# The prologue of an attention stage: another order of the first batch's work, of the stores and of the hand-over of PSUM banks

## The reference, cut to what matters

```python
x = x + attention(layernorm(x), w_in, offsets, amplitudes, sharpness)
x = x + ffn(layernorm(x), ...)
x = x + mamba(layernorm(x), ...)
x = x + ffn(layernorm(x), ...)

def attention(x, w_in, offsets, amplitudes, sharpness):   # x: 2 x 1024 x 128, 16 heads of 8
    proj = einsum('bld,ed->ble', x, w_in)
    k, v, q = heads(proj[..., :d]), heads(proj[..., d:2*d]), heads(proj[..., 2*d:])
    diff = offsets[:, :, None] - rel          # rel = -(L-1) .. L-1
    scores = sum(amplitudes * exp(-abs(sharpness) * diff * diff), axis=1)
    bias = scores[:, i - j + L - 1]
    attn = softmax(q @ k.T / sqrt(8) + bias)
    return attn @ v
```

## Time and profile before

| | us |
|---|---|
| median of 3 runs (lowest, highest) | 1184.79 (1184.17, 1186.43) |
| the profiled execution | 1184.06 |
| its span, first to last instruction | 1182.1 |
| PE busy in the span | 1020.0 |
| DVE busy | 983.5 |
| ACT busy | 719.0 |
| POOL busy | 447.7 |

### The profile page before, as it was taken

How to read it: one execution, slowest core, us unless ns; L and a number is a source line. 1 busy time by engine, 2 the same in 40 slices (tenths; PEclk the granted TensorE clock), 3 DMA queues, 4 the chain that set the end, 5 groups by cost and what they waited for, 6 DMA issues and landing times. The chain is left out here.

```text
span 1182.1 us, 19693 instructions
## 1 busy us (share of the span) xinstructions
PE 1020.0 (86%) x5756; PEld 540.9 (46%) x5756; DVE 983.5 (83%) x2432; ACT 719.0 (61%) x1175; POOL 447.7 (38%) x404
## 2 busy tenths in 40 slices
PE   3559999999999999785999999782877769999998
PEld 1212222222222222264766676541656537666775
DVE  6589999889999986168999999787876689999997
ACT  5116665666666656564777777586333537777775
POOL 4600000000000000013777778515663127777776
PEclk9659999999999999967999999986889879999999
DMA  3740122032012200000000000000000000000001
GB/s 100 255 95 8 61 76 49 16 106 66 15 55 75 57 1 2 1 21 12 20 21 18 22 18 23 3 19 0 1 0 0 21 9 21 22 18 21 19 23 38
DMA packets 56704, 41.66 MB, mean 35 GB/s; under 512 B 23334, under 2 KB 51004, under 8 KB 56636
## 3 DMA queue, kind: packets, MB, share of 16 engines
q1 hardware_dynamic: 54268, 38.18, 12.0%
q10 hardware_dynamic: 2368, 2.63, 0.8%
HBM read 33.12 MB, written 7.47 MB: 34 GB/s over the span
## 5 line engine op out<-in xcount | busy, mean ns | idle before, releaser
L514 POOL TENSOR_TENSOR f_act_low<-f_act,f_act_high 128x512 fp32r<-128x512 f32 x256 | 331.2, 1294 | 151.3 <-ACT f_act_high L471 146.3
L1203 ACT ACTIVATE at_prob<-at_cols 128x1024 f32<-128x1024 f32 x256 | 248.1, 1021 | 198.4 <-PE at_cols L1092 198.4
L1255 DVE CUSTOM_DVE_ANT_0 at_rows<-at_rows,at_table_max 128x512 f32<-128x512 f32 x512 | 340.3, 719 | 33.5 <-PE at_rows L1057 32.3
L471 ACT CAST f_act_high<-f_act 128x512 fp32r<-128x512 f32 x256 | 159.1, 621 | 68.1 <-DVE f_act L591 65.7
L585 DVE TENSOR_TENSOR f_gated<-f_relu,f_work 128x512 f32<-128x512 f32 x256 | 174.3, 681 | 21.3 <-PE f_work L417 15.1
L591 DVE TENSOR_TENSOR f_act<-f_gated,f_work 128x512 f32<-128x512 f32 x256 | 175.8, 687 | 10.2
L478 ACT ACTIVATE f_relu<-f_work 128x512 f32<-128x512 f32 x256 | 152.9, 597 | 32.1 <-PE f_work L362 30.7
L360 PE MATMUL f_work<-f_x_high,f_wu_high 128*128 128x512 f32 x256 | 148.4, 580 | 2.7 <-DVE f_wu_low L573 2.1
L1057 PE MATMUL at_rows<-at_k_stack,at_q_stack 48*128 48x512 bf16 x512 | 104.7, 405 | 39.9 <-DVE at_maxima L1255 38.4
L1104 PE MATMUL at_pv<-at_prob,at_v_stack 128*32 128x512 f32 x1024 | 136.4, 605 | 0.6 <-ACT at_prob L1203 0.6
L1092 PE MATMUL at_cols<-at_table_cols,flip_sum 128*64 128x512 f16 x1024 | 136.4, 387 | 0.0
(11 more groups left out here) (274 smaller groups left out, 1393.8 us busy)
## 6 DMA issues: line engine op xcount, KB each, us to landing
at_table_cols<-bias_rows SPq DMA_DIRECT2D x32, 248.0 KB, 5.1
at_table_max<-bias_rows SPq DMA_DIRECT2D x12, 480.0 KB, 4.3
f_wu<-in_L_ffn_up_w_dram SPq DMA_DIRECT2D x64, 64.0 KB, 2.0
f_wd<-in_L_ffn_down_w_dram SPq DMA_DIRECT2D x64, 64.0 KB, 1.8
at_q_stack<-q_parts SPq DMA_DIRECT2D x28, 96.0 KB, 2.4
at_k_stack<-k_parts SPq DMA_DIRECT2D x24, 96.0 KB, 3.9
at_table_max<-bias_rows ACTq DMA_DIRECT2D x4, 480.0 KB, 5.8
k_parts<-at_parts SPq DMA_DIRECT2D x2, 768.0 KB, 5.4
```

The costliest lines, as they stand in the source:

```text
L471: nc.scalar.copy(act_h[:, j % 4, :], act[:, j % 4, :]).then_inc(act_high, 1)
L514: nc.gpsimd.tensor_tensor(act_l[:, k, :], act[:, k, :], act_h[:, k, :].bitcast(F32), ALU.subtract).then_inc(act_low, 1)
L1203: act(prob[:, S % 2, 2 * hp:2 * hp + 2, :], s2[:, hp, :, :], ACT.Exp).then_inc(exp_done, 1)
L1255: nc.vector.tensor_tensor_reduce(out=slot, in0=slot, in1=t_max[:, 2 * p.hp + j, c:c + BANK][:, ::-1], scale=1.0, scalar=-3.0e38, op0=ALU.a ...
```

## The change

Both versions compute the same. What moves:

- The third small load (amplitudes) is issued before the weights. VectorE takes the first batch's statistics and its variance before it waits for the small loads, and normalises and copies the first batch before it takes the second batch's statistics. ScalarE takes the first root before the first square, and the first high part between the two exponentials; the second root comes after the bias.
- The first batch's parts are stored in two halves: 32 partitions (the first group's four heads) at once, the other 96 after the loads that need the first. Two of the four stores of the high bias go to SyncE's queue. The second batch's stores come after the column tables.
- The rows of ones in the k stack, filled by GpSimd before, are copied by two transfers from a small tile.
- The second batch's projections and both batches' values run between the first pairs, as twelve steps of a generator; ScalarE copies each of these projections whole and its high part, and GpSimd makes the middle and the low part. The buffers for it lie in `at_prob`, so ScalarE waits for them before the loop.
- The banks of `at_rows` are handed over one by one: each matmul of a pair waits for its own bank and increments `fills`, and each reduction waits for its own. It applies to all 256 pairs.
- The first phase's maxima are sent from ScalarE's queue.

The diff, less the renaming of `filled` and `freed` to `end`, the semaphores and the split of `RowNorm.vector_rows` in two (indentation reduced by eight):

```diff
+rest, whole = prob[:, 0, :, :], prob[:, 1, :, :]
...
-def store_piece(eng, b, kind, piece):
+def store_piece(eng, b, kind, piece, cut, out):
     at = [r for r, term in enumerate(TERMS) if term[1 - kind] == piece]
     step = at[1] - at[0] if len(at) > 1 else 1
     rows = (kd, qd)[kind][:, :, b * L:(b + 1) * L].rearrange("h (d r) l -> (h d) r l", d=HD)
-    src = parts[:, b, kind, piece, :].unsqueeze(1).broadcast_to([P, len(at), L])
-    eng.dma_start(rows[:, at[0]:at[-1] + 1:step, :], src).then_inc(stored[b], 16)
+    src = parts[cut, b, kind, piece, :].unsqueeze(1).broadcast_to([cut.stop - cut.start, len(at), L])
+    eng.dma_start(rows[cut, at[0]:at[-1] + 1:step, :], src).then_inc(out, 16)
...
+def send_maxima(eng, phase):
+    eng.wait_ge(slots_free, slots.end["maxima", phase])
+    b, lh = phase // 2 % 2, phase % 2
+    for j in range(2):
+        r = HALF * j + QK_ROWS
+        n = PIECES * HP_MAXIMA
+        eng.dma_start(q_st[r:r + PIECES, b, lh, :, :].rearrange("p h (t l) -> p (h t) l", l=P),
+                      negT[j * n:(j + 1) * n, :]).then_inc(max_in[lh], 16)
...
-        for b in range(BATCH):
-            for piece, ready in enumerate((high_ready, mid_ready, low_ready)):
-                sp.wait_ge(ready, 4 * (b + 1))
-                for kind in range(2):
-                    store_piece(sp, b, kind, piece)
-            if b == 0:
-                sp.wait_ge(stored[0], 16 * STORES)
-                sp.wait_ge(ones_made, 2)
-                load_k(sp, 0, 0, 0, L)
+        pieces = list(enumerate((high_ready, mid_ready, low_ready)))
+        for piece, ready in pieces:
+            sp.wait_ge(ready, 4)
+            for kind in range(2):
+                store_piece(sp, 0, kind, piece, slice(0, G4 * HD), stored[0])
+            if piece == 0:
+                sp.wait_ge(b_hi_ready, 1)
+                for c in range(2, 4):
+                    store_bias(sp, bias_hi, b_hi, b_hi_out, c)
+        sp.wait_ge(stored[0], 16 * STORES)
+        load_k(sp, 0, 0, 0, L)
         sp.wait_ge(b_lo_ready, 1)
         for c in range(4):
-            sp.dma_start(bias_lo[:, c * BANK:(c + 1) * BANK], b_lo[32 * c:32 * c + HEADS, :]).then_inc(b_lo_out, 16)
+            store_bias(sp, bias_lo, b_lo, b_lo_out, c)
+        for piece, _ in pieces:
+            for kind in range(2):
+                store_piece(sp, 0, kind, piece, slice(G4 * HD, P), rest_out)
+        sp.wait_ge(ones_made, 1)
+        for j in range(2):
+            r = HALF * j + QK_ROWS
+            sp.dma_start(k_st[r:r + PIECES].rearrange("p b h l -> p (b h l)").bitcast(F32)
+                         .rearrange("p (n c) -> p n c", c=P),
+                         two_ones[0:PIECES, :].unsqueeze(1).broadcast_to([PIECES, BATCH * L // P, P])
+                         ).then_inc(ones_in, 16)
         sp.wait_ge(b_hi_out, 64)
         sp.wait_ge(b_lo_out, 64)
         for c in range(CHUNKS):
             load_table(sp, 0, c)
+        for piece, ready in pieces:
+            sp.wait_ge(ready, 8)
+            for kind in range(2):
+                store_piece(sp, 1, kind, piece, slice(0, P), stored[1])
         sp.wait_ge(stored[1], 16 * STORES)
         load_k(sp, 0, 1, 0, L)
         for lh in range(2):
             load_q(sp, 0, 1, lh)
-        def send_maxima(phase):
-            sp.wait_ge(slots_free, slots.freed["maxima", phase])
-            b, lh = phase // 2 % 2, phase % 2
-            for j in range(2):
-                r = HALF * j + QK_ROWS
-                n = PIECES * HP_MAXIMA
-                sp.dma_start(q_st[r:r + PIECES, b, lh, :, :].rearrange("p h (t l) -> p (h t) l", l=P),
-                             negT[j * n:(j + 1) * n, :]).then_inc(max_in[lh], 16)
-        send_maxima(0)
+        sp.wait_ge(rest_out, 16 * STORES)
...
-        pool.wait_ge(norms[1].norm, LT)
-        for j in range(2):
-            rows = k_st[HALF * j + 32:HALF * (j + 1)].rearrange("p b h l -> p (b h l)")
-            nc.gpsimd.memset(rows.bitcast(F32), TWO_ONES).then_inc(ones_made, 1)
-        pool.wait_ge(ones_made, 2)
+        nc.gpsimd.memset(two_ones[:], TWO_ONES).then_inc(ones_made, 1)
...
-            low_part(n)
+            pool.wait_ge(high_ready, n + 1)
+            tt(whole[:, n % 4, :], whole[:, n % 4, :], part(n, 0), ALU.subtract).then_inc(rest_ready, 1)
+            pool.wait_ge(rest_ready, n - 3)
+            nc.gpsimd.tensor_copy(part(n, 1), whole[:, n % 4, :]).then_inc(mid_ready, 1)
+            pool.wait_ge(mid_ready, n + 1)
+            tt(part(n, 2), whole[:, n % 4, :], part(n, 1), ALU.subtract).then_inc(low_ready, 1)
...
+        def project(n):
+            pe.wait_ge(xnT_ready, n // 2 + 1)
+            mm(proj_bank(n), wT[:, (0, 2)[n % 2], :], xnT[:, n // 2 * BANK:(n // 2 + 1) * BANK],
+               start=True, stop=True).then_inc(proj_done, 1)
         turn_rows(0)
...
-        project(0)
-        project(1)
+        for n in range(KINDS // 2):
+            project(n)
...
-        pe.wait_ge(xnT_ready, NQ)
-        for g in range(NQ):
-            values(g)
-        project(2)
-        project(3)
+        def second_batch():
+            for n in range(KINDS // 2, KINDS):
+                pe.wait_ge(proj_read, n - 3)
+                project(n)
+                yield
+            for g in range(NQ):
+                if g:
+                    pe.wait_ge(high_ready, KINDS // 2 + g)
+                for k in range(QT):
+                    t = g * QT + k
+                    last = mm(v_bank(g)[:, k * P:(k + 1) * P], xnT[:, t * P:(t + 1) * P], wT[:, 1, :],
+                              start=True, stop=True)
+                    if k % 2 == 1:
+                        if k == QT - 1:
+                            last.then_inc(v_done, 1)
+                        yield
         def rows_pair(n):
             p, at = Pair(n), slots.start["pair", n]
             if n % (2 * PHASE_PAIRS) == 0:
                 pe.wait_ge(stack_in[p.b], stack_count(p.g))
-            if at + 2 > SLOTS:
-                pe.wait_ge(slots_free, at + 2 - SLOTS)
             for j in range(2):
                 r = slice(HALF * j, HALF * j + QK_ROWS)
-                last = mm(s1[:, (at + j) % SLOTS, :], q_st[r, p.b, p.lh, p.hp, p.lbq * P:(p.lbq + 1) * P],
-                          k_st[r, p.b, p.hp, p.mh * BANK:(p.mh + 1) * BANK], start=True, stop=True)
-            last.then_inc(fills, 1)
+                if at + j >= SLOTS:
+                    pe.wait_ge(slots_free, at + j + 1 - SLOTS)
+                mm(s1[:, (at + j) % SLOTS, :], q_st[r, p.b, p.lh, p.hp, p.lbq * P:(p.lbq + 1) * P],
+                   k_st[r, p.b, p.hp, p.mh * BANK:(p.mh + 1) * BANK], start=True, stop=True).then_inc(fills, 1)
...
-        pe.wait_ge(v_copied, NQ)
+        pe.wait_ge(xnT_ready, NQ)
+        pe.wait_ge(b_lo_ready, 1)
+        more = second_batch()
         for n in range(AHEAD):
             rows_pair(n)
+            if n:
+                next(more, None)
             if n + 1 == TURN_FIRST_AFTER:
                 pe.wait_ge(m.turn_made, TURN_MADE)
                 turn_maxima(0)
-        pe.wait_ge(proj_read, KINDS)
+        for _ in more:
+            pass
+        pe.wait_ge(v_copied, NQ)
+        pe.wait_ge(high_ready, KINDS)
+        pe.wait_ge(ones_in, 32)
...
-        for t, src in ((off, offsets), (shp, sharpness)):
+        for t, src in ((off, offsets), (shp, sharpness), (amp, amplitudes)):
...
+        norms[0].scalar_root(a)
         a.wait_ge(signs, 3)
         square(0)
-        norms[0].scalar_root(a)
         a.wait_ge(w_turned, 1)
         nc.scalar.copy(wT[:, 0:2, :].rearrange("p a d -> p (a d)"), pv[:, 0:2 * D]).then_inc(w_ready, 1)
         nc.scalar.mul(wT[:, 2, :], pv[:, 2 * D:3 * D], 1.0 / math.sqrt(HD)).then_inc(w_ready, 1)
         square(1)
-        norms[1].scalar_root(a)
-        for g in range(HG):
-            gaussian(g)
-        for n in range(KINDS // 2):
+        gaussian(0)
+        high_part(0)
+        gaussian(1)
+        for n in range(1, KINDS // 2):
             high_part(n)
         a.wait_ge(bias_ready, 1)
-        nc.scalar.copy(b_hi[:], s1[:, 0, :]).then_inc(b_hi_ready, 1)
+        nc.scalar.copy(b_hi[:], s1[:, 2, :]).then_inc(b_hi_ready, 1)
         a.wait_ge(b_hi_ready, 1)
-        for c in range(4):
-            a.dma_start(bias_hi[:, c * BANK:(c + 1) * BANK], b_hi[32 * c:32 * c + HEADS, :]).then_inc(b_hi_out, 16)
-        for g in range(NQ):
-            a.wait_ge(v_done, g + 1)
-            bank = (s1[:, 1, :], s1[:, 2, :], pv[:], s1[:, 0, :])[g]
-            nc.scalar.copy(v_nat[:, g * QT:(g + 1) * QT, :].rearrange("p t d -> p (t d)"), bank).then_inc(v_copied, 1)
+        for c in range(2):
+            store_bias(a, bias_hi, b_hi, b_hi_out, c)
+        norms[1].scalar_root(a)
+        a.wait_ge(b_hi_out, 64)
+        load_max_tables(a, 0, 0)
         a.wait_ge(stored[0], 16 * STORES)
         for lh in range(2):
             load_q(a, 0, 0, lh)
-        a.wait_ge(b_hi_out, 64)
-        for hp in range(2):
```

(57 more changed lines are left out.)

74 lines of the change are left out of this document (29 added, 45 removed).

## The result

The changed kernel takes 1176.2 us (median of 9 runs, 1173.12 to 1181.07) against 1184.97 for the kernel before on the same chip (9 runs, 1183.92 to 1189.67): a ratio of 0.9928, 95% interval 0.9906 to 0.9949. It is faster by 8.8 where 16.0 were forecast, and lies 0.2 outside the range of 1164 to 1176. The profiled execution took 1175.85 with a span of 1173.8, against 1182.1: 8.3 less.

What follows compares the result with a forecast made beforehand. Only attention's prologue was taken to move: the chain to the first score reduction, then VectorE-paced pairs ahead of the loop. Gains 13.3 + 2.7 = 16.0 took the profiled 1184.06 to 1168.1, median 1168.8; range 1164 to 1176.

Steps and rivals of the forecast that it cites:

- landed 28.0: Attention prologue: the last store ahead of the q loads lands at 28.0, against 34.01 before, taking 2.8 after issue.
- the chain up to the last store: Prologue, statistics to last store issued at 25.2; last low part at 24.75 instead of 29.68, 4.9 gained.
- The hole of 0.17 a pair: Pairs ahead of the loop: single-bank hand-over closes TensorE's wait, taking a pair from 1.47 to 1.30.
- Work costed at nothing in the prologue: Second batch's parts on GpSimd, SyncE's extra stores and fills, ScalarE's copies and maxima transfers: covered, zero cost.
- The loop's pace: Attention loop of 128 steps: a wait and increment per matmul cost zero; pair to pair stays 3.05.
- Dear increments: Rival, chance 0.08: a second increment per pair delays the hand-over, adding 7 over 234 loop pairs: 1176.
- the first exponential at 75.51 in place of 67: Start of the attention loop: its first exponential was forecast near 67.
- I take 33.0: Prologue: the q stack lands at 33.0, bounds 30.5 to 36.5; first reduction 33.7, gaining 13.3.
- Stalls at the projections 1.5: Pairs ahead of the loop: two or three projections run at the low clock, costing 1.5, bounds 0 and 3.4.
- 44 of them are 28.4, the maxima's pieces and their copy about 1.4: Stretch ahead of the loop: 44 reductions at 0.65 each plus maxima work; with stalls 31.3 against 34.0, gaining 2.7.
- GpSimd's work covered: Second batch's middle and low parts on GpSimd end near 52, and even doubled before the loop that waits for them.
- late stacks: Rival, chance 0.17: tables, k and q stacks collide, first reduction at 37.2, all projections run slow: 1174.2.

Runs made afterwards that it cites:

- e3: Changed kernel with the old hand-over of PSUM banks by pairs restored (one wait, one increment of two per pair): 1179.59 us, 0.9942 of the kernel before.
- e5: Changed kernel, but SyncE sends the stores of the remaining heads only after the first stacks have landed: 1177.43 us, 0.9922 of the kernel before.
- e6: Changed kernel with ScalarE's q loads issued ahead of both maximum tables on its queue: 1177.85 us, 0.9933 of the kernel before.
- n1: Changed kernel, but second maximum tables and stores of the remaining heads wait until the first stacks have landed: 1177.11 us, 0.9933 of the kernel before.
- e4: Changed kernel with the second batch's four projections issued before the first pair, not between pairs: 1177.0 us, 0.9927 of the kernel before.
- e1: Changed kernel, but GpSimd waits for the first phase's maxima before making the later stages' constants (its selects): 1173.6 us, 0.9906 of the kernel before.
- e2: Changed kernel plus a one-column exponential on ScalarE after it sends the maxima, loading the table in idle time: 1177.47 us, 0.9933 of the kernel before.
- f2: f1 plus e2's early load of the exponential's table: 1175.58 us, 0.9913 of the kernel before.
- f1: Changed kernel with e1's edit, plus three repeats of part of the product (48 rows) after each pair from the fifteenth: 1177.25 us, 0.9922 of before.
- f3: f2 with the three extra products per pair on all 128 rows and columns of the array instead of 48 rows: 1170.13 us, 0.9872 of before.
- m1: Changed kernel plus only f3's three full-array products after each pair from the fifteenth, without e1's and e2's edits: 1179.96 us, 0.9949 of before.

## Why the prediction was half right

**Right, by its own steps.** Variance 8.0 (7.87), root done 8.3 (8.11), first high part 16.05 (15.59), last low part 24.75 (23.97), last store issued 25.2 (24.36) and landed 28.0 (26.1, 1.7 after issue): the chain up to the last store came in 0.1 to 0.8 earlier than worked out, the landing 1.9. The hole of 0.17 a pair closes, but e3 prices it at 1.7 and not at the 3.7 of 22 pairs, because for about half of the pairs the clock was high, where the old hand-over has no hole (1.30 a pair in e3). Work costed at nothing in the prologue mostly cost nothing: the rest stores (e5), the second batch's parts, the maxima on ScalarE's queue. The loop's pace is unchanged. "Dear increments" had the number nearest to the result, 1176, and that is luck: the mechanism isn't there. The rule cited for it, in the Trainium skill's "TensorE: Matmul & The Clock Gate", section "The cost: per-tile semaphore tail", may hold where increments bound the stream; here 234 more of them cost nothing that a trace shows (0.23 and 3.06 in the steady step, and e3 without them no shorter: 401.9 behind the first three steps, for 401.6 to 401.7).

**Wrong, with what each term measured** (the first exponential at 75.51 in place of 67):

- "I take 33.0" for the q stack: 34.9, although its stores were in 1.9 sooner. The first reduction is 1.95 late. The term was mis-sized, within its bounds; what sets it are the tables and stacks themselves, and neither their order nor what is sent behind them (e5, e6, n1).
- Stalls at the projections 1.5: 2.4 (1.29, 0.87 and two of 0.11), 0.9 more. e4 moves them and gains nothing.
- "44 of them are 28.4, the maxima's pieces and their copy about 1.4": this step failed. It took the pieces at their duration in the old trace, where GpSimd's selects, at 53.44, were long done when VectorE negated at 70.75. The change brings VectorE forward by 11 and GpSimd's selects back by 7, onto each other: 3.8 (e1). The prediction called GpSimd's work covered because its results are ready before the loop waits for them; that it can stop VectorE was not asked.
- The second root was moved behind the last exponential of the prologue, and what it leaves behind was not followed: the loop's first exponential loads its table again, 1.28 (e2, and f2 against f1). The sum has no term for it.
- From scores to first exponential, without the table, 0.4 more than before, at the low clock.

Together 1.95 + 0.9 + 3.8 + 1.3 + 0.4 = 8.4, and the loop is 0.8 shorter than before (410.71, 411.48): 7.6, against the 7.7 missing in the span (16.0 - 8.3). The next rival, "late stacks" (1174.2), has a mechanism that is there, but it accounts for only 1.95 and the 0.9 of the stalls.

The removal of a cost didn't return its price. e1 won 3.75 and kept 1.45; with the clock held (f3) collision, table load and clock together return 4.5 of the 5.1 of the first two at the last exponential (486.51 to 482.05), from a first reduction 0.9 later.

**Open**: why the granted clock is back at 73 to 76 in some profiled runs and at 78 to 84 in others, with TensorE busy nearly throughout (e1: 9.47 of 10.00 at 0.50), and so how much of the changed kernel's spread (1173 to 1181) it makes. m1's spans (1174.1 to 1180.8) suggest that there the negation meets one select or two, but only one run has a trace.

## What to carry to other kernels

When a change moves one engine's work by ten microseconds, go through what every other engine then does beside it, not only who waits for whom: here two engines that exchange nothing collided. Follow the state that a moved instruction leaves (ScalarE's table) to its next user. And measure a repair at the end of the loop as well as at its start, for TensorE's clock may take the gain back.
